# A decoder layer with attention and experts: shared expert and padding rows inside the second stage's last steps, and routing of two batches per operation

## The chip, the cores and the metric

The kernel runs on one core of one Trainium2 chip. The metric is the device time of one execution in microseconds, the median over runs. TensorE (PE), VectorE (DVE), ScalarE (ACT), GpSimd (POOL) and the sync engine (SP, which issues transfers) each work through their own list of instructions in order and wait for each other by semaphores.

## The reference

Sixteen batches of 128 tokens with 256 features go through three blocks, each with a residual and a layer norm: self-attention (linear and windowed, gated), cross-attention with 16 heads on a context of 128 tokens, and a mixture of experts. The last one is what the change is about:

```
logits = tokens @ router_weight.T;  scores = sigmoid(logits);  sfc = scores + router_bias
group_scores = top2 sum of sfc in each of 4 groups of 8 experts;  keep the best 2 groups
topk_idx = top 4 of the kept sfc;  topk_w = scores[topk_idx] / sum * 2.5
mixed  = sum over the 4 chosen experts of topk_w * down(silu(gate(token)) * up(token))
shared = (silu(x @ shared_gate.T) * (x @ shared_up.T)) @ shared_down.T
x = layernorm(x + mixed + shared)
```

There are 32 experts with an inner width of 128; the shared expert has an inner width of 256.

## The kernel before, in words

The program has three stages, with a barrier of all engines and a clearing of semaphores between them. Every float32 product is made of three float16 products (high x high, high x low, low x high), so a value is split into a `_hi` part (a copy by ACT) and a `_lo` part (a subtraction by DVE or POOL).

**Stage 1** (self-attention) is not touched.

**Stage 2** (`cross_attention`) is a software pipeline over the 16 batches (`NB`). Each engine has a loop over steps `i`, and in each step it calls a fixed list of functions, each for the batch `i` minus a lag of its own: the order of this list is the order of the engine's instructions. PE has 23 steps, DVE 21, ACT 23, POOL 25, SP 23; DVE's step i runs together with about PE's step i + 2. A batch's way through the stage: `x1_T`, `q_proj`, `k_proj`, `v_proj`, `scores`, `mins` (a row minimum on DVE, L1333), `exps` (ACT, L1259), `transposed`, `pT_high` and `p_low` (L1339), `weighted`, `out_proj`, `st` (layer norm statistics, DVE, L1379), `pow_` (POOL), `x2` (L1388), then `xhl_high` and `xhl_low`, the transpose `x2_T`, `logits` and `logits_exp` (ACT), and on DVE the routing: `scores_` (L1395 to L1397), `groups` (L1403 to L1407), `picks` (L1414 to L1417), `chosen` (L1425 to L1429, the selection `selc`), `weights` (L1435 to L1439), after PE's `counts` (running numbers within each expert, by a matmul with a triangle of ones) `places` (L1446 to L1448), `slots_` (L1455 to L1458) and `payload` (L1464 to L1467, the last instruction for a batch). POOL then sends the 128 rows of the batch to the memory `x_rows` of the four chosen experts, in four indirect transfers (`scatter`, L1191). Each DVE routing step waits for the one before it through a semaphore (`chain`). ACT uses Exp and Copy here.

PE's products share seven PSUM banks; the table `ORDERS` says who follows whom in each bank, and `Turns.wait` makes PE wait until the previous content of the bank has been read.

**Stage 3** (`expert_layer`). SP first reads the final row of each of the 32 experts from `fill_row` into registers and writes one block of 128 padding rows behind each expert's rows (L1738, 32 transfers from `padrow`). It then waits for the scatters and the pads and gathers blocks of rows `xg` (L1755, 96 tiles, 20 buffers). Meanwhile PE, ACT and DVE compute the shared expert in 8 chunks of two batches (`shared_chunk`): gate and up products over 256 columns (L1934), SiLU on ACT (L1796), the product `shid` (L1867), its halves `sh_hi` (ACT, L1799) and `sh_lo` (DVE, L1871), the down product, and the sum into `xs` (L1876). Between chunk 0 and 1 PE builds with one matmul (L1956) the table which tile belongs to which expert, from a chain of some 19 small DVE instructions (up to L1855). Then come the 96 expert tiles: transposes (L1985), gate and up (L1934 again, 12 matmuls over 128 columns), down (L1995), the weighting on DVE (L1886), an indirect transfer by POOL (L1772), and at the end the final sums and the last layer norm.

## Time and profile before

| | |
|---|---|
| median of 3 runs | 803.7 us (801.82 to 803.7) |
| the profiled execution's own time | 802.68 us |
| its span (first to last instruction) | 800.9 us |
| mean granted TensorE clock | 0.866 of full speed |
| stage 1 | 0 to 270.9 us |
| stage 2 | 270.9 to 557.9 us |
| stage 3: shared expert | 557.9 to 599.2 us |
| stage 3: expert tiles and final sums | 599.2 to 800.9 us |
| PE, DVE, ACT, POOL busy | 78%, 73%, 66%, 67% of the span |

Times in the trace are microseconds from the span's start. An engine's busy time is the union of its instructions' durations; what a row gives in brackets is the idle time of the engine just before it and the instruction that ended it. PEclk is the TensorE clock that was granted, 1.00 for 2.4 GHz and 0.50 for 1.2 GHz, averaged over the stretch.

### The profile page before, as it was taken

How to read it: one execution, taken by the hardware profiler on the slowest of the kernel's cores; microseconds unless marked ns; L12 is line 12 of the kernel's file. 1: busy time of each engine (PE TensorE's matmuls, PEld its weight loads, DVE VectorE, ACT ScalarE, POOL GpSimd, SP SyncE). 2: the span in 40 equal slices, each digit the busy share in tenths (PEclk: the TensorE clock that was granted, in tenths of full speed). 3: DMA queues.
4: the chain of work that ended last, by engine and by line, in shares of the span. 5: the costliest groups of instructions: out<-in, count | busy, mean ns of one | idle time of the engine just before them, and what ended most of it. 6: DMA issues, size and time to landing. Idle time of an engine off the chain costs nothing. (4 is left out here: it accounts for less than half of the span.)

```text
span 800.9 us, 24293 instructions
## 1 busy us (share of the span) xinstructions
PE 624.3 (78%) x7778; PEld 518.9 (65%) x7778; DVE 586.5 (73%) x2170; ACT 524.8 (66%) x1542; POOL 533.2 (67%) x689
## 2 busy tenths in 40 slices
PE   3899999999998488878777888631889999999100
PEld 2688888888888366756666666421679887777100
DVE  5898888888885367999999999882546655555495
ACT  5699999898887299878787787520228765555000
POOL 5877989999898535477767766663004765556684
PEclk9899999999999789787978787655899999999655
DMA  9200000000000122333543354241942555452383
GB/s 323 64 19 2 2 3 14 21 3 3 2 2 4 46 73 68 100 114 115 147 125 119 116 155 129 93 151 55 211 135 79 148 161 154 142 170 85 139 271 117
DMA packets 57131, 77.68 MB, mean 97 GB/s; under 512 B 8488, under 2 KB 46512, under 8 KB 56880
## 3 DMA queue, kind: packets, MB, share of 16 engines
q1 hardware_dynamic: 46208, 56.37, 24.7%
q0 software_dynamic: 7680, 16.87, 5.8%
q10 hardware_dynamic: 3120, 2.88, 1.1%
q8 instruction: 67, 1.10, 0.6%
q14 instruction: 56, 0.46, 0.2%
HBM read 44.39 MB, written 27.49 MB: 90 GB/s over the span
## 5 line engine op out<-in xcount | busy, mean ns | idle before, releaser
L1772 POOL DMA_INDIRECT y_rows<-yo,xg x96 | 94.7, 986 | 98.2 <-DVE yo L1886 60.0
L1886 DVE TENSOR_SCALAR yo<-bank,xg 128x256 f32<-128x256 f32 x96 | 46.4, 484 | 57.2 <-PE bank L1995 56.7
L1259 ACT ACTIVATE scx<-bank,mnx 128x128 f32<-128x128 f32 x256 | 73.9, 408 | 18.9 <-DVE mnx L1333 18.7
L1934 PE MATMUL bank<-gT,we_hi 128*128 128x128 f16 x768 | 79.1, 219 | 4.5 <-DVE eh L1896 3.6
L500 ACT ACTIVATE sc<-sc,mn 128x128 f32<-128x128 f32 x256 | 79.6, 396 | 0.0
L1191 POOL DMA_INDIRECT x_rows<-rows,slot_ix x64 | 63.5, 992 | 21.6 <-issue 18.3
L1162 POOL TENSOR_TENSOR we_lo<-east,we_hi 128x256 f16<-128x256 f32 (+1 forms) x80 | 59.3, 768 | 11.4 <-ACT we_hi L1233 11.1
L1934 PEld LDWEIGHTS bank<-gT,we_hi 128*128 (+1 forms) x768 | 51.8, 96 | 19.9 <-issue 9.9
L674 DVE CUSTOM_DVE_ANT_0 sc<-bank,rel 128x128 f32<-128x128 f32 x256 | 57.8, 286 | 8.7 <-PE bank L783 8.6
L1808 ACT ACTIVATE gT<-bank 128x512 f16<-128x512 f16 x96 | 56.4, 591 | 7.9 <-PE bank L1985 7.7
L1813 ACT ACTIVATE eh_hi<-eh 128x128 f16<-128x128 f32 x96 | 29.7, 309 | 46.8 <-DVE eh L1896 46.2
L1564 PE MATMUL bank<-ident,scx 128*128 128x128 f32 x256 | 51.5, 340 | 2.9 <-ACT scx L1259 2.8
L1934 PE MATMUL bank<-gT,we_lo 128*128 128x128 f16 x384 | 53.1, 218 | 0.0
L1339 DVE TENSOR_TENSOR pTx_lo<-bank,pTx_hi 128x512 f16<-128x512 f32 x64 | 43.6, 681 | 5.2 <-ACT pTx_hi L1267 4.8
L683 DVE TENSOR_TENSOR pT_lo<-bank,pT_hi 128x512 f16<-128x512 f32 x64 | 43.1, 681 | 5.0 <-ACT pT_hi L507 4.9
L830 PE MATMUL bank<-hT,w_hi 128*128 128x128 f16 x384 | 42.6, 227 | 3.3 <-DVE q_lo L655 2.3
L1333 DVE TENSOR_REDUCE mnx<-bank 128x4 f32<-128x512 f32 x64 | 42.5, 673 | 1.1 <-DVE rows L1458 0.3
L507 ACT ACTIVATE pT_hi<-bank 128x512 f16<-128x512 f32 x64 | 37.9, 592 | 6.8 <-PE bank L805 5.0
L1267 ACT ACTIVATE pTx_hi<-bank 128x512 f16<-128x512 f32 x64 | 40.0, 632 | 1.9 <-PE bank L1564 1.8
L793 PE MATMUL bank<-ident,sc 128*128 128x128 f32 x256 | 40.0, 279 | 0.4 <-ACT sc L500 0.4
L1564 PEld LDWEIGHTS bank<-ident,scx 128*128 128x128 f32 x256 | 35.4, 174 | 4.6 <-ACT scx L1259 4.6
L1985 PE MATMUL bank<-ident,xg 128*128 128x128 f16 x384 | 36.6, 218 | 1.6 <-DVE xs L1876 0.8
(291 smaller groups left out, 2441.6 us busy)
## 6 DMA issues: line engine op xcount, KB each, us to landing
xg<-x_rows SPq DMA_DIRECT2D x96, 129.0 KB, 2.6
east<-in_experts SPq DMA_DIRECT2D x32, 384.0 KB, 3.5
rows<-xhl SPq DMA_DIRECT2D x16, 512.0 KB, 4.5
yg<-y_rows SPq DMA_DIRECT2D x16, 512.0 KB, 4.5
x_rows<-padrow SPq DMA_DIRECT2D x33, 129.0 KB, 4.1
wst<-in_wcat SPq DMA_DIRECT2D x8, 256.0 KB, 5.6
cst<-in_ctx_t SPq DMA_DIRECT2D x16, 128.0 KB, 3.3
out<-fin ACTq DMA_DIRECT2D x16, 128.0 KB, 3.1
```

The lines of the kernel that those rows point to most:

```text
L500: done = act.activation(sc[:, g, j], sc[:, g, j], ACT.Exp, bias=mn[:, n % 2, g, j:j + 1], scale=-1.0)
L674: dve.tensor_tensor_reduce(out=sc[:, g, j], in0=sc_bank[g][:, j * P:(j + 1) * P], in1=rel[:, g, j], scale=-1.0, scalar=-NEG, op0=ALU.add, ...
L683: dve.tensor_tensor(pT_lo[:, g % 2], pT_bank[g][:].rearrange("p (h k) -> p h k", h=GH), pT_hi[:, g % 2], ALU.subtract).then_inc(pT_rd[g], 1)
L1162: pool.tensor_tensor(pair(shared.we_lo, piece, n), arrived(piece), pair(shared.we_hi, piece, n), ALU.subtract).then_inc(we_lo_done[k], 1)
L1191: pool.indirect_dma_start(shared.x_rows, bass.IndirectOffsetOnAxis(ap=slot_ix[:, n, k:k + 1], axis=0), rows4[:, q, k], None).then_inc(shar ...
L1259: done = act.activation(scx[:, g, j], sc_bank[g][:, j * P:(j + 1) * P], ACT.Exp, bias=mnx[:, n % 2, g, j:j + 1], scale=-1.0)
L1339: dve.tensor_tensor(pTx_lo[:, g % 2], pT_bank[g][:].rearrange("p (h k) -> p h k", h=GH), pTx_hi[:, g % 2], ALU.subtract).then_inc(xpT_rd[g ...
L1564: last = pe.transpose(pT_bank[g][:, j * P:(j + 1) * P], scx[:, g, j], ident[:])
L1772: pool.indirect_dma_start(c.y_rows, bass.IndirectOffsetOnAxis(ap=xg_word(U32, n % G, 0), axis=0), yo[:, n % YO], None, bounds_check=NDEST ...
L1808: act.activation(gT[:, n % U], GT_BANK[n % len(GT_BANK)], ACT.Copy).then_inc(gt_r, 1)
L1886: dve.tensor_scalar(yo[:, n % YO], DN_BANK[n % 2][:, 0:D], xg_word(F32, n % G, 1), None, ALU.mult).then_inc(yo_r, 1)
L1934: done = pe.matmul(o[:, m * width:(m + 1) * width], lhs(x_, k, m), rhs(y_, k, m), start=t == 0, stop=t == 5)
```

## The change

**Shared expert.** The 8 chunks move from the start of stage 3 into the last steps of stage 2, as functions in the lists of the engines: on PE `sh_in` (gate and up, one batch at a time, so over 128 columns) in steps 17 to 24 and `sh_out` (down) in steps 18 to 25; on ACT `sh_gate` and `sh_high`, on DVE `sh_mult`, `sh_low` and `sh_add`. They use three PSUM banks that other uses leave free by then. `shid`, `sh_hi` and `sh_lo` have one buffer each instead of two. PE's loop now has 26 steps, ACT's 27, DVE's 25, POOL's 26.

**Padding.** `fill_row` is computed on DVE in its step 20, after the last `places`; SP issues 16 of the 32 padding transfers after its loop in stage 2, and ACT the other 16 after its own. SP in stage 3 waits for them before the first gather, as before.

**Routing.** The DVE functions from `scores_` to `payload` run once for two batches, in every second step, with both batches in one instruction where the instruction allows it. MAX8 and MATCH_REPLACE stay one per batch. `counts` on PE does five matmuls per pair instead of four per two batches. `scatter` on POOL runs one step later. The group mask is no longer an operation of its own, and the sum of the weights is.

**Table.** In stage 3, PE's matmul for the tile table now stands in the tile loop, in step 5, ahead of the gate and up product of tile 1 and behind the transposes of tile 4.

Cut to its core:

```diff
-                for i in range(NB + 7):
+                def sh_in(n, b):
+                    if live(n, NCH):
+                        wait_turn(pe, f"GU{b}", n)
+                        for j, col in enumerate((C_SG, C_SU)):
+                            for m in range(KT):
+                                t = 0
+                                for x_, y_ in ((0, 0), (1, 0), (0, 1)):
+                                    for k in range(KT):
+                                        done = pe.matmul(gate_up(b, j)[:, m], W[x_][:, k, col + m * P:col + (m + 1) * P], shared.xT[:, 2 * n + b, y_, k],
+                                                         start=t == 0, stop=t == 5)
+                                        t += 1
+                        done.then_inc(filled[f"GU{b}"], 1)
+                def sh_out(n):
+                    if live(n, NCH):
+                        H = (sh_hi, sh_lo)
+                        wait_turn(pe, "SD", n)
+                        pe.wait_ge(shlo_r, n + 1)
+                        products("SD", lambda s, k, m: H[s][:, m, k], lambda s, k, m: W[s][:, k, C_SD:C_SD + D], 2, D)
+                for i in range(NB + 10):
...
                     x1_T(i)
+                    sh_in(i - FIRST_SH, 0)
                     transposed(i - 3, 0)
                     k_proj(i - 2)
+                    sh_out(i - FIRST_SH - 1)
                     transposed(i - 3, 2)
                     q_proj(i - 1)
+                    sh_in(i - FIRST_SH, 1)
...
+                for i in range(NB + 11):
                     ao_high(i - 6)
                     pT_high(i - 5, 2)
+                    sh_high(i - FIRST_SH - 2)
...
                     x1T_(i - 1)
+                    sh_gate(i - FIRST_SH - 1, 0)
                     xq_high(i - 2)
+                    sh_gate(i - FIRST_SH - 1, 1)
+                pad_rows(act, mybir.EngineType.Activation, 1)
...
-                for i in range(NB + 5):
-                    chosen(i - 5)
+                for i in range(NB + 9):
+                    sh_mult(i - FIRST_SH + 1, 0)
                     xq_low(i)
                     p_low(i - 2, 2)
+                    sh_mult(i - FIRST_SH + 1, 1)
                     xv_low(i - 1)
+                    sh_add(i - FIRST_SH)
                     mins(i - 1, 1)
                     weights(i - 5)
                     places(i - 5)
+                    if i == NB + 4:
+                        dve.tensor_scalar(shared.fill_row[:], shared.count[:], -1.0, None, ALU.add).then_inc(shared.fill_r, 1)
                     mins(i - 1, 0)
+                    sh_low(i - FIRST_SH + 1)
                     scores_(i - 4)
...
+                    chosen(i - 4)
...
+        def pad_rows(eng, kind, part):
+            eng.wait_ge(shared.fill_r, 1)
...
+            for v in rows:
+                eng.dma_start(shared.x_rows[bass.ds(v, P), :], shared.padrow[:]).then_inc(shared.filled, 16)
...
                 def tile(i, s, h):
+                    if i == L_GU + 1:
                         pe.wait_ge(tab_step, TAB_STEPS)
                         pe.matmul(TAB_BANK[:, 0:2 * P], c.ones[:], diag[:].rearrange("p s t -> p (s t)"), start=True, stop=True).then_inc(tab_ps, 1)
```

DVE's list in the steady part of stage 2, where a batch gets its weights (`wraw` to `wt`) and its places (`slots`, `ykey`), before:

```order
L1435 SCALAR_TENSOR_TENSOR wraw,wsum<-cout,score 128x32
L1437 TENSOR_SCALAR wsum<-wsum 128x1
L1438 RECIPROCAL winv<-wsum 128x1
L1439 TENSOR_SCALAR wt<-wraw,winv 128x32
L1446 TENSOR_TENSOR slots<-bank,count 128x32
L1447 TENSOR_TENSOR count<-bank,count 128x32
L1448 TENSOR_TENSOR ykey<-slots,selc 128x32
```

and the same place now, in every second step:

```order
L1485 SCALAR_TENSOR_TENSOR wraw<-cout,score 128x64
L1486 TENSOR_REDUCE wsum<-wraw 128x2
L1487 TENSOR_SCALAR wsum<-wsum 128x2
L1488 RECIPROCAL winv<-wsum 128x2
L1489 SCALAR_TENSOR_TENSOR wt<-wraw,winv 128x64
L1495 TENSOR_TENSOR slots<-bank,count 128x64
L1497 TENSOR_TENSOR count<-bank,count 128x32
L1498 TENSOR_TENSOR ykey<-slots,selc 128x64
```

Seven instructions for each batch have become eight for two, over 64 columns where it was 32.

ACT's list in one of the last steps of stage 2, now (L1328 is the SiLU of the shared expert, L1335 its high half, L1322 the exponential of the logits); before, the stage had no table load:

```order
L1311 ACTIVATE xhl<-xs 128x256
L1328 ACT_TABLE_LOAD
L1328 ACTIVATE shid<-bank 128x256
L1328 ACTIVATE shid<-bank 128x256
L1335 ACTIVATE sh_hi<-shid 128x512
L1316 ACTIVATE hT<-bank 128x512
L1322 ACT_TABLE_LOAD
L1322 ACTIVATE rt_e<-bank 128x32
```

Exp and Silu take turns here. There are nine such loads in the stage's last steps.

PE's list at the start of stage 3, now:

```order
L2016 MATMUL bank<-ident,xg 128x128
L2016 MATMUL bank<-ident,xg 128x128 x3
L1994 MATMUL bank<-diag,ones 128x256
L1984 MATMUL bank<-gT,we_hi 128x128
```

These are the transposes of tile 4, the table's matmul and the first gate product of tile 1; before, the table's matmul stood ahead of the second chunk of the shared expert, and 8 chunks ahead of the first tile.

## Rows read from the trace of the kernel before

**Rows 1.** The page: span

```profile
span 800.9 us, 24293 instructions
```

**Rows 2.** Busy time by stretch (us; engine busy, instructions; PEclk; DMA share; GB/s)

```profile
core 0: us, PE busy (x) PEld busy (x) DVE busy (x) ACT busy (x) POOL busy (x), PEclk, DMA share, GB/s
303.06:315.05 11.99, 10.62 (x144) 8.24 (x141) 8.10 (x19) 11.45 (x36) 7.04 (x12) 0.86 0.30 79
341.44:498.21 156.77, 124.71 (x1466) 99.49 (x1462) 144.42 (x502) 120.16 (x364) 109.28 (x148) 0.79 0.43 129
...
518.00:529.00 11.00, 5.35 (x46) 3.61 (x42) 8.61 (x40) 3.05 (x7) 8.03 (x10) 0.66 0.52 167
529.00:551.00 22.00, 2.82 (x18) 2.39 (x18) 13.94 (x72) 1.21 (x3) 14.86 (x17) 0.50 0.27 96
...
558.00:570.00 12.00, 8.51 (x42) 5.95 (x43) 6.24 (x25) 2.58 (x4) 0.07 (x1) 0.67 0.74 177
570.00:599.00 29.00, 27.52 (x251) 24.14 (x248) 14.66 (x23) 8.45 (x14) 0.00 (x0) 1.00 0.71 167
```

**Rows 3.** DVE in order of time, 487 to 546 (start us, us)

```profile
489.66 0.43 DVE L1379 BATCH_NORM_STATS2 xstats<-bank 128x6 f32<-128x256 f32 x1
...
517.99 0.43 DVE L1379 BATCH_NORM_STATS2 xstats<-bank 128x6 f32<-128x256 f32 x1 [0.77 <-PE bank L1508]
...
528.60 0.43 DVE L1379 BATCH_NORM_STATS2 xstats<-bank 128x6 f32<-128x256 f32 x1 [1.11 <-PE bank L1508]
...
545.26 0.29 DVE L1467 TENSOR_REDUCE rows<-wpick 128x4 f32<-128x128 f32 x1
```

**Rows 4.** In order of time: the ends of stage 2 and of stage 1

```profile
550.15 0.96 POOL L1191 DMA_INDIRECT x_rows<-rows,slot_ix  x1 [0.30 <-issue]
557.94 0.12 POOL L1768 MEMSET cums<- 128x32 f32 x1 [6.83 <-POOLq L963]
...
268.80 0.41 DVE L734 TENSOR_SCALAR xs<-yt,mv,rstd 128x256 f32<-128x256 f32 x1 [0.75 <-POOL rstd L326]
270.94 0.23 POOL L1144 MEMSET xv_hi<- 128x32 f16 x1 [2.18 <-POOLq L946]
```

**Rows 5.** PE in order of time, 566 to 603

```profile
566.43 1.22 PE L1956 MATMUL bank<-diag,ones 128*128 128x256 f32 x2 [3.49 <-DVE diag L1855]
...
572.29 0.60 PE L1934 MATMUL bank<-hT,w_hi 128*128 128x256 f16 x4
...
576.22 0.60 PE L1934 MATMUL bank<-hT,w_hi 128*128 128x256 f16 x4
...
600.62 0.39 PE L1934 MATMUL bank<-gT,we_hi 128*128 128x128 f16 x4
...
601.29 0.39 PE L1985 MATMUL bank<-ident,xg 128*128 128x128 f16 x4
...
602.18 0.39 PE L1985 MATMUL bank<-ident,xg 128*128 128x128 f16 x4
```

**Rows 6.** SP's queue in order of time

```profile
559.71 17.96 SPq L1738 DMA_DIRECT2D x_rows<-padrow  x32
582.55 9.37 SPq L1755 DMA_DIRECT2D xg<-x_rows  x20
```

**Rows 7.** Groups of DVE instructions, 341.44 to 498.21 (busy us, mean ns, idle before)

```profile
L1395 DVE TENSOR_SCALAR rt_e<-rt_e 128x32 f32<-128x32 f32 x10 | 5.6, 560 | 0.0
L1464 DVE TENSOR_TENSOR wpick<-ykey,y 128x128 f32<-128x128 f32 x10 | 5.5, 547 | 0.0
...
L1396 DVE RECIPROCAL score<-rt_e 128x32 f32<-128x32 f32 x10 | 3.5, 353 | 0.3
```

**Rows 8.** In order of time: table load, and the last chunk's low half

```profile
557.94 1.28 ACT L1796 ACT_TABLE_LOAD   x1 [21.33 <-PEq L963]
...
596.20 0.69 DVE L1871 TENSOR_TENSOR sh_lo<-shid,sh_hi 128x512 f16<-128x512 f32 x1 [0.69 <-ACT sh_hi L1799]
```

**Rows 9.** The page: DMA issues (KB each, us to landing)

```profile
xg<-x_rows SPq DMA_DIRECT2D x96, 129.0 KB, 2.6
```

More of the change, by code:

```diff
@@ L31 @@
 PIECES = ((0, 1, 2), (3, 4))
+NCH = NB // 2
+FIRST_SH = 17
 ROUTE_SCALE = 2.5
@@ L81, in live, with pair_done @@
     return 0 <= n < count
+def pair_done(n):
+    return live(n) and n % 2 == 1
 def unrolled(lag, step, count=NB):
@@ L100, in wait @@
                 tile = i + k // len(order) - self.lags[prev]
-                if 0 <= tile < NB:
-                    pe.wait_ge(self.emptied[prev], self.reads.get(prev, 1) * (tile + 1))
+                each = self.every.get(prev, 1)
+                if 0 <= tile < self.counts.get(prev, NB) and (tile + 1) % each == 0:
+                    pe.wait_ge(self.emptied[prev], self.reads.get(prev, 1) * (tile + 1) // each)
                     break
@@ L1106, in arrived @@
             return east[:, k, at:at + 2 * EI * (1 + piece // 4)].rearrange("p (h w) -> p h w", w=2 * EI)
+        def pad_rows(eng, kind, part):
+            eng.wait_ge(shared.fill_r, 1)
+            _, rows = nc.values_load_multi_w_load_instructions(
+                shared.fill_row[0:1, part * NE // 2:(part + 1) * NE // 2], engines=[kind], min_val=0, max_val=NE * CAP - P,
+                skip_runtime_bounds_check_because="an expert's rows start at a multiple of CAP and are at most CAP - P")
+            for v in rows:
+                eng.dma_start(shared.x_rows[bass.ds(v, P), :], shared.padrow[:]).then_inc(shared.filled, 16)
         with nc.Block() as block:
@@ L1138, in _ @@
                     context(i)
+                pad_rows(sp, mybir.EngineType.SP, 0)
             @block.gpsimd
@@ L1204, in _ @@
                     ao_low(i - 5)
-                    scatter(i - 8, 0)
+                    scatter(i - 9, 0)
             @block.scalar
@@ new lines, in places @@
+                def places(n):
+                    if pair_done(n):
+                        link = chain(dve, place_step, PLACE_STEPS, n // 2)
+                        dve.wait_ge(filled["CN"], n // 2 + 1)
+                        link(dve.tensor_tensor(slots[:], room["CN"][:, 0:2 * NE].rearrange("p (s e) -> p s e", s=2),
+                                               shared.count[:].unsqueeze(1).to_broadcast([P, 2, NE]), ALU.add))
+                        dve.tensor_tensor(shared.count[:], room["CN"][:, 2 * NE:3 * NE], shared.count[:], ALU.add).then_inc(emptied["CN"], 1)
+                        link(dve.tensor_tensor(ykey[:], slots[:], selc[:], ALU.mult))
+                        dve.wait_ge(emptied["CN"], n // 2 + 1)
@@ new lines, in slots_ @@
+                def slots_(n):
+                    if pair_done(n):
+                        start = SLOT_STEPS * (n // 2)
+                        for s in range(2):
+                            dve.max(y8[:, s], ykey[:, s]).then_inc(slot_step, 1)
+                        dve.wait_ge(slot_step, start + 2)
+                        dve.tensor_scalar(slot_ix[:, n - 1:n + 1], y8[:, :, 0:TOPK], -1.0, None, ALU.add).then_inc(slot_step, 1)
+                        for b in (n - 1, n):
+                            wait(dve, shared.scattered[b % RR], 16 * TOPK * (b // RR))
+                            dve.tensor_copy(rows4[:, b % RR, :, D:D + 1], dest_f[:, b].unsqueeze(2)).then_inc(slot_step, 1)
@@ new lines, in sh_mult, with sh_low @@
+                def sh_mult(n, b):
+                    if live(n, NCH):
+                        dve.wait_ge(emptied[f"GU{b}"], 2 * n + 1)
+                        dve.tensor_tensor(shid[:, b], gate_up(b, 1), shid[:, b], ALU.mult).then_inc(emptied[f"GU{b}"], 1)
+                def sh_low(n):
+                    if live(n, NCH):
+                        dve.wait_ge(shhi_r, n + 1)
+                        wait(dve, filled["SD"], n)
+                        dve.tensor_tensor(sh_lo[:], shid[:], sh_hi[:], ALU.subtract).then_inc(shlo_r, 1)
@@ L1730, in _ @@
                 sp.dma_start(known[:], consts[:, 2 * P + NE:2 * P + 2 * NE + 1]).then_inc(k_in, 16)
-                sp.wait_ge(fill_r, 1)
-                for half_ in range(2):
-                    _, rows = nc.values_load_multi_w_load_instructions(
-                        fill_row[0:1, half_ * NE // 2:(half_ + 1) * NE // 2], engines=[mybir.EngineType.SP], min_val=0, max_val=NE * CAP - P,
-                        skip_runtime_bounds_check_because="an expert's rows start at a multiple of CAP and are at most CAP - P")
-                    for v in rows:
-                        sp.dma_start(c.x_rows[bass.ds(v, P), :], c.padrow[:]).then_inc(filled, 16)
                 for q in range(RR):
@@ L1827, in _ @@
             def _(dve):
-                dve.tensor_scalar(fill_row[:], c.count[:], -1.0, None, ALU.add).then_inc(fill_r, 1)
                 link = chain(dve, tab_step, TAB_STEPS, 0)
```

264 lines of the change are left out of this document (115 added, 149 removed).

## The prediction

> **What bounds the kernel now.** I read the page first, then the stretches by stage, then in each stage the engine that never waits. The profiled execution took 802.7 us around a span of 800.9 us [rows 1]; the median of the three runs is 803.7 us, so 1 us above what the sums below start from. An effect of 0.3%, 2.4 us, is about what a measurement of this kernel can tell from none.
>
> In the steady part of the second stage DVE is busy 144.4 of 156.8 us, ACT 120.2, PE 124.7, POOL 109.3, and the TensorE clock is granted at 0.79 on average, so PE spends part of it at 1.2 GHz [rows 2]. Ten batches pass there, one per 15.7 us. In the one batch period before any routing (303.06 to 315.05) the time is 12.0 us, DVE busy 8.1 and ACT 11.45 [rows 2]. So two limits are seen: with routing DVE sets 15.7 us, without it ACT sets 12.0 us. DVE's attention work is those 8.1 us, some 7.8 where it runs without a pause and neighbours overlap; the rest of the 15.7 us, 7.9, is routing: 30 small instructions, 0.26 us apiece with the gaps.
>
> The end of that stage is a chain of latencies: PE is busy 5.4 of 11 us, then 2.8 of 22 us, at a clock of 0.66 and 0.50 (1.2 GHz) [rows 2]. Batch 12's statistics start at 489.66, batch 15's at 528.60, the last payload instruction ends at 545.55 [rows 3], POOL's last scatter issues at 550.15, and the third stage starts at 557.94, after 6.83 us of POOL idle [rows 4]. In contrast the first stage ended 269.21 (DVE) and the second began at 270.94, only 1.7 us later [rows 4]; so some 5 of the 6.8 us belong to POOL's indirect transfers being the last thing, not to the barrier.
>
> The third stage begins with the shared expert, which is PE's: 27.5 of 29 us busy at full clock [rows 2], one chunk per 3.93 us (572.29 to 576.22), and the experts' sixth tile (number 5) begins at 602.18, 44.2 us into the stage [rows 5]. The pads (18 us of issue from 559.71) and the first gathers (from 582.55) lie under it [rows 6]. The stage's rest is not touched.
>
> **1. Routing of two batches per operation.** Per pair 60 DVE instructions become 42, since everything except MAX8, MATCH_REPLACE and a few writes is issued once over 64 columns. What goes once instead of twice, by the mean durations [rows 7]: the add after the exponential (0.56 us), the comparison for the payload (0.55), and their like. What gets wider costs by columns: the reciprocal over 64 instead of 32 columns, if proportional, 0.70 for 0.35; the other instructions gain about 0.03 us for 32 columns more. MAX8 stays. Written out for the eight groups (scores 1.6, groups 1.4, picks 1.1, chosen 1.4, weights 1.4, places 0.8, slots 0.9, payload 1.8) a pair costs 10.4 us instead of 15.8; by mere count, 42 at 0.26, it is 11.1. I take 10.8, a saving of 2.5 us per batch, bounds 2.3 and 2.7. The scores to chosen groups fall on one iteration and weights to payload on the next, about 5.4 us each, so there is no heavy and light iteration. DVE's floor becomes 13.2 us per batch, ACT's is 12.0. Two engines that close will wait for each other: I take 13.6 us, a gain of 2.1 us over 11 periods (from batch 4 to the first shared work): **-23 us**. Bounds: nothing below 12.9 us (gain 30), and if coupling eats most, 15 us (gain 8).
>
> **2. The tail.** PE's loop goes from 23 to 26 iterations, with a chunk's gate and up products in iterations 17 to 24 and its down product one later. PE's work per chunk is still 3.9 us at full clock. The gate and up products are now 48 matmuls over 128 columns instead of 24 over 256; the experts do 12 of those in 0.67 us (600.62 to 601.29) [rows 5], thus 2.7 us for 48; a chunk's 36 matmuls over 256 columns took 3.93 us, 0.109 each, thus 2.6 us for the 24. The Trainium skill (TensorE: Matmul & The Clock Gate, Back-to-back issue gap) gives about 81 ns per matmul at 128 columns because each needs its weight load, and by that a chunk would be 1.2 us longer and the tail up to 10 us; the trace has 56 ns here, so the sum goes without it.
>
> The iterations, counted from the statistics of batch 12 (iteration 17): 17 and 18 still carry full attention, plus 4 us of PE work, minus the cheaper routing: 15.5 and 15 us (28.3 for both before, from 489.66 to 517.99 [rows 3]). 19 to 22 carry the last routing chain and a chunk side by side: 13, 10, 9 and 8 (before 10.6, and 17 us for the rest up to 545.55). 23 and 24, and the start of 25, are a chunk's chain alone: sh_low 0.69, out 1.3, gate and up half 1.35, SiLU 0.4, product 0.4, sh_hi about the same as sh_low, and about 1 us of hops: near 6 each (SiLU and product are estimates, half of an operation of sh_low's width and a bit) [rows 5, 8]. Up to the last sh_high that is about 82 us.
>
> ACT must switch between Exp and Silu: nine table loads in the tail where the stage had none, 1.28 us each [rows 8], 11.5 us on an engine that is busy only 3.1 of 11 and 1.2 of 22 us there [rows 2]; about half fall on the chain and are in the iteration times. The Trainium skill (ScalarE: Activation LUTs, What ACT_TABLE_LOAD costs) counts 2.66 us for a switch with its drain, and advises to group work by set, against this change; by it the tail would be another 6 us longer. The trace's own load stands alone at the stage's start, 1.28 us and then a wait for PE, so it shows no drain; 6 us more stay inside the forecast's own range.
>
> The padding rows: their numbers exist after the last count (DVE iteration 20). SP has nothing left and issues 16 in 9 us under chunks 5 to 7, at 17.96/32 = 0.56 us apiece with the register loads [rows 6]. ACT's 16 stand behind its last sh_high and nothing covers them: 16 x 0.56 = **9 us**, taking ACT to issue as fast as SP, while sh_low, the down product and the add need 3. So ACT ends the stage, 82 + 0.6 + 9, about 92 us after batch 12's statistics. POOL scatters batches 14 and 15 together, 8 x (0.96 + 0.30) = 10 us [rows 4], plus its 5 us of draining, but starts at about 66 and is done by 82: hidden, so the exit costs 2 us and not 6.8. Tail: 94 us against 68.3 now: **+26 us**. Bounds +16 (iterations near 6 us from 20 on) and +42.
>
> **3. The third stage's head.** No shared expert, and no wait for the pads. SP gathers at once; landing takes 2.6 us [rows 9]. But PE now waits before tile 5 for the table that DVE builds: its matmul started 8.5 us into the stage, and takes 1.2 us [rows 5]. So tile 5 begins at 9.7 us instead of 44.2: -34.5. PE comes out of a pause and has the 1.2 GHz clock for the first 8 us or more, as it had from 558 to 569 (mean 0.67 up to 570, then 1.00 [rows 2]); tiles of 1.2 us then take 2.4: +4. **-30.6 us**, bounds -27 and -34. Gathers go out every 0.47 us (9.37/20) [rows 6] and stay ahead.
>
> Sum: 802.7 - 23 + 26 - 30.6 = **775 us**.
>
> **Rivals.**
> *Coupling keeps the period near 15.* For it: ACT is at 12.0 us per batch, PE at 12.5 with half its time at the low clock, POOL at 11 with in-order scatters; against it: the 12.0 us period with ACT at 95%. Gain 8 instead of 23: 790 us. Chance 0.17.
> *Clock in the tail stays at 1.2 GHz.* For it: 0.66 and 0.50 there [rows 2]. Each chunk's 2.7 us in the chain double; over the last iterations +10: 785 us. Against: added matmuls make PE denser. Chance 0.15.
> *Both cheap.* Period 13.0 (-30) and a tail of +20: 762 us. Chance 0.10.
> *Slower: the tail runs serially.* ACT and DVE are in-order queues, and one waiting SiLU holds the routing behind it. If a chunk's chain (5.8, with slow clock 8.5) and two table loads (2.6) add fully to iterations 17 to 22, 67 us, and three bare chunks follow at 8.5, then the tail is 55.9 + 67 + 25.5 + 11.5 = 159 us for 68.3, and the kernel 840 us. It decides from 54 us of growth instead of 26, or 3.1 us more in each of nine iterations. Against it: ACT and PE are nearly idle there, and chunks are put one iteration apart. Chance 0.06, and 0.02 for just balancing.
> *Forecast, 766 to 784*: 0.50.
>
> **How the numbers follow.** Time 775 us, the likeliest case. Range 760 to 793: it takes in the first three rivals and leaves out the serial one and the extreme of the cheap one. Faster 0.92, same 0.02, slower 0.06, since only the serial case brings back the 54 us of steps 1 and 3.
>
> **What would show it.** Right: statistics of neighbouring batches 13 to 14 us apart between 340 and 480; DVE waiting at times, for ACT or PE; the third stage starting at about 557.9 - 23 + 26 = 561; ACT's pad issues last before it, with POOL idle; the experts' sixth tile under 15 us after the stage's start. Wrong: a period over 15, table-load pairs with ACT full in the tail, stage start after 575, or a first gather that waits for the pads.

## The result and the profile after

The changed kernel takes 769.79 us (768.49 to 772.76, 4 runs) against 802.88 us (801.82 to 803.7, 4 runs) for the kernel before: a ratio of 0.9594, 95% interval 0.9561 to 0.9626. The forecast was 775 us, the range 760 to 793. All ratios leave out two runs far from the others, one of the kernel before (1775.5 us) and one of the routing alone (909.07 us, clock 0.70). The profiled execution took 770.42 us around a span of 768.6 us:

```profile
span 768.6 us, 24515 instructions
```

Busy time by stretch of the changed kernel: the steady part, four stretches of the tail up to the last payload, the chunks alone, the wait for the pads, and the third stage's head. They answer to [rows 2].

```profile
core 0: us, PE busy (x) PEld busy (x) DVE busy (x) ACT busy (x) POOL busy (x), PEclk, DMA share, GB/s
343.50:469.80 126.30, 102.11 (x1356) 82.63 (x1358) 112.71 (x353) 109.32 (x335) 96.09 (x129) 0.92 0.46 139
469.80:488.80 19.00, 15.25 (x188) 12.54 (x186) 13.96 (x53) 15.49 (x41) 13.58 (x19) 0.80 0.45 140
488.80:505.60 16.80, 14.08 (x170) 12.33 (x170) 10.86 (x27) 11.73 (x29) 7.86 (x10) 0.72 0.25 79
505.60:517.00 11.40, 8.60 (x109) 7.41 (x108) 8.95 (x44) 6.97 (x13) 6.98 (x10) 0.92 0.37 118
517.00:535.80 18.80, 15.46 (x184) 13.89 (x183) 15.24 (x68) 8.12 (x13) 12.46 (x14) 0.87 0.37 131
535.80:549.00 13.20, 9.36 (x140) 8.62 (x136) 5.58 (x11) 3.81 (x8) 7.85 (x8) 1.00 1.01 228
549.00:559.70 10.70, 1.47 (x12) 1.10 (x12) 1.38 (x2) 0.00 (x0) 0.00 (x0) 0.83 0.87 193
559.70:570.20 10.50, 5.38 (x46) 4.59 (x47) 5.17 (x23) 2.85 (x6) 0.12 (x1) 0.52 0.69 172
```

In the steady part DVE is busy 89% (before 92%) and ACT 87% (before 77%): no engine is full any more. The tail, where PE was busy 2.8 of 22 us, now has PE at four fifths, and the 1.2 GHz clock (0.50) is gone from it. At the very end nearly nothing computes for 10.7 us while the transfer engines stay at 0.87.

The same by instructions in order of time, as [rows 3]: DVE's statistics of batches 13, 14 and 15, the last payload instruction, and the last addition of the shared expert.

```profile
488.83 0.43 DVE L1421 BATCH_NORM_STATS2 xstats<-bank 128x6 f32<-128x256 f32 x1 [0.28 <-PE bank L1585]
505.62 0.43 DVE L1421 BATCH_NORM_STATS2 xstats<-bank 128x6 f32<-128x256 f32 x1
517.01 0.43 DVE L1421 BATCH_NORM_STATS2 xstats<-bank 128x6 f32<-128x256 f32 x1 [0.60 <-PE bank L1585]
535.27 0.48 DVE L1521 TENSOR_REDUCE rows<-wpick 128x4 f32<-128x128 f32 x2
551.37 0.69 DVE L1537 TENSOR_TENSOR xs<-bank,xs 128x512 f32<-128x512 f32 x1 [1.65 <-PE bank L1585]
```

POOL's, ACT's and SP's queues around the border of the stages, as [rows 4, 6]:

```profile
545.59 0.96 POOL L1216 DMA_INDIRECT x_rows<-rows,slot_ix  x1 [0.31 <-issue]
559.70 0.12 POOL L1851 MEMSET cums<- 128x32 f32 x1 [13.16 <-POOLq L971]
...
549.77 8.16 ACTq L1130 DMA_DIRECT2D x_rows<-padrow  x16
...
534.71 9.05 SPq L1130 DMA_DIRECT2D x_rows<-padrow  x16
562.65 10.08 SPq L1838 DMA_DIRECT2D xg<-x_rows  x20
```

And PE at the start of stage 3, as [rows 5]: the transposes of tiles 0 to 3, the table's matmul, and tile 5.

```profile
564.82 2.07 PE L2016 MATMUL bank<-ident,xg 128*128 128x128 f16 x16 [13.49 <-DMA xg<-x_rows]
...
568.39 1.17 PE L1994 MATMUL bank<-diag,ones 128*128 128x256 f32 x2
...
570.22 0.39 PE L2016 MATMUL bank<-ident,xg 128*128 128x128 f16 x4
```

With the statistics of batch 12 at 469.80 (before 489.66), the span divides as follows (us). The first two result columns are the profiled executions of the kernel before and of the changed one; the two after them are the parts alone, of the experiments below.

| stretch | before | changed | routing alone | shared expert alone |
|---|---|---|---|---|
| up to the statistics of batch 12 | 489.7 | 469.8 | 468.9 | 488.1 |
| from there to batch 15's | 38.9 | 47.2 | 41.2 | 49.9 |
| from there to stage 3 | 29.3 | 42.7 | 33.4 | 44.8 |
| stage 3 up to tile 5 | 44.2 | 10.5 | 43.0 | 10.0 |
| the rest | 198.7 | 198.4 | 199.1 | 198.5 |

So -19.9, then +21.7 in the tail (from batch 12's statistics to stage 3), then -33.7 in the head (stage 3 up to tile 5): 32 us.

### The profile page after: what moved, and what is told of

Its sections match the earlier page's. It is cut to its first block and busy times, and to the rows that moved or that the text cites. A ratio compares the mean times of both kernels' runs of the same rounds, so it can differ in the third digit from the quotient of the medians.

```text
span 768.6 us, 24515 instructions
## 1 busy us (share of the span) xinstructions
PE 610.7 (79%) x7986; PEld 513.5 (67%) x7986; DVE 552.5 (72%) x2018; ACT 534.4 (70%) x1558; POOL 534.5 (70%) x689
## 5 line engine op out<-in xcount | busy, mean ns | idle before, releaser
L1936 DVE TENSOR_SCALAR yo<-bank,xg 128x256 f32<-128x256 f32 x96 | 46.4, 484 | 57.1 <-PE bank L2028 57.0
L1187 POOL TENSOR_TENSOR we_lo<-east,we_hi 128x256 f16<-128x256 f32 (+1 forms) x80 | 59.5, 769 | 11.7 <-ACT we_hi L1258 11.5
L1381 DVE TENSOR_TENSOR pTx_lo<-bank,pTx_hi 128x512 f16<-128x512 f32 x64 | 43.7, 682 | 10.5 <-ACT pTx_hi L1292 10.4
L1641 PE MATMUL bank<-ident,scx 128*128 128x128 f32 x256 | 46.4, 311 | 2.9 <-ACT scx L1284 2.3
L2016 PEld LDWEIGHTS bank<-ident,xg 128*128 128x128 f16 x384 | 24.4, 98 | 18.2 <-DMA xg<-x_rows 14.1
```

Of the source, the lines that this page charges most:

```text
L1187: pool.tensor_tensor(pair(shared.we_lo, piece, n), arrived(piece), pair(shared.we_hi, piece, n), ALU.subtract).then_inc(we_lo_done[k], 1)
L1381: dve.tensor_tensor(pTx_lo[:, g % 2], pT_bank[g][:].rearrange("p (h k) -> p h k", h=GH), pTx_hi[:, g % 2], ALU.subtract).then_inc(xpT_rd[g ...
L1641: last = pe.transpose(pT_bank[g][:, j * P:(j + 1) * P], scx[:, g, j], ident[:])
L1936: dve.tensor_scalar(yo[:, n % YO], DN_BANK[n % 2][:, 0:D], xg_word(F32, n % G, 1), None, ALU.mult).then_inc(yo_r, 1)
L2016: done = pe.transpose(GT_BANK[n % len(GT_BANK)][:, part, k], xg[:].bitcast(F16)[:, n % G, (part * KT + k) * P:(part * KT + k + 1) * P], c. ...
```

## The experiments

Twelve kernels ran, in three groups. The first four ran on a chip where the kernel before takes 801.03 us; the next four and the last four on two other chips, where it takes 865.93 and 865.83 us. The record does not name the chip of the result above; the kernel before takes 802.88 us there, and "the first chip" below means both. Between those chips and the first only ratios, or differences within a group, are compared. Each diff is against the changed kernel unless it says otherwise.

### Each part alone

The first kernel has the paired routing alone (no `sh_` functions, pads and shared expert in stage 3 as before), the second the move of the shared expert, pads and table alone (routing per batch).

```diff
-                    sh_in(i - FIRST_SH, 0)
-                    sh_out(i - FIRST_SH - 1)
-                    sh_in(i - FIRST_SH, 1)
...
-                pad_rows(sp, mybir.EngineType.SP, 0)
...
-                pad_rows(act, mybir.EngineType.Activation, 1)
```

and the second:

```diff
-                    if pair_done(n):
-                        link = chain(dve, score_step, SCORE_STEPS, n // 2)
+                    if live(n):
+                        s = n % 2
+                        link = chain(dve, score_step, SCORE_STEPS, n)
```

> Only the routing of two batches per operation, shared expert and pads where they were. My theory (DVE sets the steady period, so its saving is time): the period falls from 15.7 to about 13.8 us as in the changed kernel, batch 12's statistics come some 20 us earlier; at the end POOL has eight scatters behind the last payload instead of four (8 x 1.26 instead of 4 x 1.26 us), which gives back about 4.5 us of it: 803 - 20 + 4.5 = 787 us. Rival A (the gain of the steady part needs the rest of the change, or is lost again in the stage's end): 797 us or more. Rival B (no loss at the end): 783.

> Only the move of the shared expert, the pads and the tile table; routing one batch at a time. My theory (the two parts add): stage 3's head gains 33.7 us as in the changed kernel, the stage's end grows by about 24 us (21.6 measured with pairs, and some 2.5 us more of DVE work in each of a few iterations, less the four scatters that POOL has less): 803 - 33.7 + 24 = 793 us, with batch 12's statistics still at about 489.7. Rival (the chunks only fit because paired routing made room on DVE): the end grows by 34 us or more, 803 us or slower.

Measured: routing alone 788.38 us, ratio 0.9851 (0.9824 to 0.9877); shared expert alone 795.04 us, ratio 0.9924 (0.9895 to 0.9953). Both are near what was expected, and they save 12.6 and 6.0 us, 19 together, where the whole change saves 33. The table above shows where the parts don't add. Routing alone makes the tail 6.4 us longer than before, shared expert alone makes it 26.5 longer: 33 together, but the whole change pays only 22. The end of the routing alone, by stretch:

```profile
468.90:486.70 17.80, 14.74 (x140) 11.43 (x138) 12.66 (x51) 11.87 (x36) 13.58 (x19) 0.62 0.47 150
486.70:498.60 11.90, 10.32 (x107) 7.88 (x104) 8.62 (x23) 8.03 (x24) 7.25 (x10) 0.50 0.33 104
498.60:510.10 11.50, 6.69 (x53) 4.96 (x50) 7.50 (x41) 3.05 (x7) 8.46 (x11) 0.50 0.44 145
510.10:526.00 15.90, 3.22 (x20) 2.80 (x20) 11.03 (x58) 1.21 (x3) 11.35 (x13) 0.50 0.39 132
```

PE runs at or near 1.2 GHz (0.50) throughout; the kernel before had 0.84, 0.50, 0.66 and 0.50 in its four stretches between the same instructions. Also its last eight scatters, of two batches, come after the last payload (526.03 to 536.64, stage 3 at 543.48) and hold the exit; before, they ended 5.6 us after it. In the whole change they lie under the chunks. From this I took the slow clock to be the cause of the longer end, and tested it (below).

### The table loads

```diff
-                        act.activation(shid[:, b], gate_up(b, 0), ACT.Silu).then_inc(emptied[f"GU{b}"], 1)
+                        act.activation(shid[:, b], gate_up(b, 0), ACT.Copy).then_inc(emptied[f"GU{b}"], 1)
```

The shared expert's SiLU is left out, so ACT needs no table but that of Exp, and the nine loads are gone.

> The changed kernel with a plain copy for the SiLU of the shared expert, in the same places and widths (this leaves out the shared expert's SiLU): no change of tables in the second stage, one load at the start of the third. My theory (nine loads of 1.28 us, about half of them on the chain): 770 - 5.5 = 764 us. Rival A, by the Trainium skill (ScalarE: Activation LUTs, What ACT_TABLE_LOAD costs: 2.66 us per switch with its drain): 11 us or more less, 759. Rival B (ACT waits there anyway, loads are hidden): 770.

Measured: 769.49 us, ratio 0.9615 (0.9579 to 0.9651), for 0.9594 (0.9561 to 0.9626) with the loads. The nine loads together cost nothing that can be measured; by the two intervals the cost is at most some 2 us, so the 5.5 us of the theory are excluded, a load or two on the chain is not. One of the loads in the changed kernel, on ACT:

```profile
502.42 0.59 ACT L1304 ACTIVATE aT<-bank 128x512 f16<-128x512 f16 x1
503.02 1.28 ACT L1322 ACT_TABLE_LOAD   x1
504.32 0.20 ACT L1322 ACTIVATE rt_e<-bank 128x32 f32<-128x32 f32 x1
```

The load starts at the end of the instruction before it, takes 1.28 us, and the next one follows at once; no drain beside it is seen, so the 2.66 us of the Trainium skill (ScalarE: Activation LUTs, What ACT_TABLE_LOAD costs) are not what this trace shows. This load is on the chain that ended last, which the profile follows back to 499.48 and which goes from ACT's `aT` through the load to the exponential and DVE's routing:

```profile
503.02 0.36 ACT L1322
```

It is the only one of the six loads after 499.48 that the chain touches. The others fall where something else was later; ACT is busy 42.3 of the 66.0 us from batch 12's statistics to the last payload, with the loads. The traces agree on the size: from batch 12's statistics to the end of the last `sh_high` it is 79.2 us with the loads and 78.0 without.

### Who issues the padding

```diff
+                pad_rows(sp, mybir.EngineType.SP, 1)
-                pad_rows(act, mybir.EngineType.Activation, 1)
```

> The changed kernel with all 32 padding transfers on SP (16 more behind its own 16) and none on ACT. My theory (ACT's issue behind its last work ends the stage): ACT's 16 issues end at 557.93, DVE's last add at 552.06; SP's issues would run from 534.7 to about 552.7, so the third stage starts at about 554.5 instead of 559.7, and the table chain, not the gathers, sets its start: 770 - 5 = 765 us. Rival (the DMA engines, fully busy from 536 to 549, land the pads no earlier, and the first gather still waits for them until about 562): 769 to 770 us, stage 3 starting earlier but its first tile not.

Measured: 767.49 us, ratio 0.9582 (0.9536 to 0.9628), between the two expectations and indistinguishable from the changed kernel. SP issued all 32 from 535.35 to 555.36 (0.62 us each instead of 0.57), stage 3 began 2.2 us earlier, but SP still waited until 560.95 for the landing, so the first gather left only 1.7 us earlier. The chain that ended last in the changed kernel says the same from its side: PE's last chunk, then ACT's pad issues (left out here), then the landing of pads, then the first gather.

```profile
544.59 1.47 PE bank L1585 x12
546.07 1.35 PE bank L1705 x24
...
557.59 4.98 DMA x_rows<-padrow
562.65 2.13 DMA xg<-x_rows
```

The pads back in stage 3, all on SP after the barrier:

```diff
-                pad_rows(sp, mybir.EngineType.SP, 0)
...
-                pad_rows(act, mybir.EngineType.Activation, 1)
...
+                sp.wait_ge(c.fill_r, 1)
+                for half_ in range(2):
...
+                    for v in rows:
+                        sp.dma_start(c.x_rows[bass.ds(v, P), :], c.padrow[:]).then_inc(c.filled, 16)
```

> The changed kernel with all 32 padding transfers back at the start of stage 3, on SP; the shared expert stays in stage 2. Theory (the pads must leave stage 3 with the shared expert that hid them): stage 3 starts about 5 us earlier, at 554, since ACT issues nothing after its last work; then 18 us of issue and 5 us of landing stand alone before the first gather, at about 578; tile 5 begins near 585 instead of 570: 769 + 14 = 783 us. Rival (gathers overlap the pads enough, or the table chain hides most): under 776.

Measured on the second chip: 862.46 us, ratio 0.9962 (0.9946 to 0.9979): almost the whole gain is gone, somewhat more than expected. Stage 3 begins at 583.69, the pads take SP from 585.47 to 603.46, the first gather leaves at 609.80 and tile 5 begins at 617.23, 33.5 us into the stage. Without the shared expert over them, pads in stage 3 stand bare; the move of the pads is what makes the move of the shared expert pay.

Pads split 26 to 6, with two semaphores (the first 16 gathers wait for the first 16 pads), and `known` loaded in stage 2:

```diff
-                pad_rows(sp, mybir.EngineType.SP, 0)
+                pad_rows(sp, mybir.EngineType.SP, 0, 16)
+                pad_rows(sp, mybir.EngineType.SP, 16, 26)
...
-                pad_rows(act, mybir.EngineType.Activation, 1)
+                pad_rows(act, mybir.EngineType.Activation, 26, 32)
...
-                sp.wait_ge(c.filled, 16 * NE)
+                sp.wait_ge(c.filled[0], 16 * 16)
...
+                    if n == 16:
+                        sp.wait_ge(c.filled[1], 16 * 16)
```

> A version meant to beat the change: SP issues 26 of the pads and ACT 6; two semaphores, so that the first 16 gathers (first blocks of experts 0 to 15) wait for the pads of these 16 experts alone; and the constants of the table are loaded in stage 2. Theory (ACT's issue and the wait for landed pads are on the path): stage 3 starts at about 555 instead of 559.7, gathers go out at once, the table is ready 5.5 us into the stage instead of 8.5, and tile 5 begins at about 563 instead of 570.2: 769 - 7 = 762 us. Rival, after e4 (the DMA engines' rate is the limit, gathers queue behind the pads): first tiles land near 562 as before, 767 us.

Measured on the second chip: 836.25 us, ratio 0.9685 (0.9653 to 0.9718). There was no run of the changed kernel beside it, so it was run again in the last group.

### Does DVE still set the period?

```diff
-                        dve.tensor_tensor(wpick[:], ykey[:].unsqueeze(2).to_broadcast([P, 2, TOPK, NE]),
-                                          y8[:, :, 0:TOPK].unsqueeze(3).to_broadcast([P, 2, TOPK, NE]), ALU.is_equal).then_inc(pay_step, 1)
...
-                        dve.tensor_tensor(wpick[:], wpick[:], wt[:].unsqueeze(2).to_broadcast([P, 2, TOPK, NE]), ALU.mult).then_inc(pay_step, 1)
```

> The changed kernel without the two products of the payload step (comparison and weighting, 0.50 + 0.81 us per pair); the tokens' weights in the rows are then something else. It asks what sets the steady period now. Theory 1 (DVE still does): the period falls by 0.65 us from 13.8 to 13.1, batch 12's statistics come 7 us earlier: 762 us. Theory 2 (ACT, with 12.5 of 13.8 us busy, and the waits between ACT, DVE and POOL do): 2 us or less, 767 or more.

This kernel leaves out the comparison and the weighting, so the weights that go with the tokens are wrong. Measured on the second chip: 846.02 us, ratio 0.9786 (0.9759 to 0.9812), the statistics of batch 12 at 484.2, as in the two kernels before it (485.9 and 483.7). Removing 1.3 us of DVE work per pair gives nothing there: the statistics stand 15.1 and 16.0 us apart in turn with it and without. The same steady stretch, of this kernel:

```profile
359.00:470.40 111.40, 87.93 (x1057) 73.10 (x1058) 86.34 (x289) 84.08 (x257) 79.62 (x110) 0.79 0.42 127
```

DVE is busy 78% there, ACT 75%, PE 79% at a granted clock of 0.79. On the first chip the changed kernel has a period of 13.75 us and a clock of 0.92. So on the second chip DVE does not bound this part; that PE does so through its clock fits, but wasn't tested, and on the first chip this kernel did not run. What sets the period of 13.75 us there was not tested either.

### Is it the clock that makes the end slow?

The paired routing alone, with idle products of the shared expert's shape in PE's steps from 17 on (their results are read by nobody). Against the routing alone:

```diff
+                def filler(i):
+                    if i >= 17:
+                        for j, col in enumerate((C_SG, C_SU)):
...
+                                        pe.matmul(room["XT"][:, j * D:j * D + P], W[x_][:, k, col + m * P:col + (m + 1) * P], shared.xT[:, i - 17, y_, k],
+                                                   start=t == 0, stop=t == 11)
...
+                    filler(i)
```

> Paired routing alone (e1) with idle matmuls: in PE's steps 17 to 22 twice 24 matmuls over 128 columns whose result nobody reads, as much work as the gate and up products of a chunk. My theory, new: in e1 the clock falls to 1.2 GHz from 469 us on (0.62, then 0.50) and what DVE waits for there is PE; the shared expert's work in the changed kernel holds the clock at 0.72 to 0.92. Then the filler's own 2.7 us per step are paid back by the clock: granted clock over 0.75 in the stage's end, time from batch 12's to batch 15's statistics 38 us or less instead of 41.2, whole kernel 3 us or more faster than e1 (788), at 785 or less. Rival (latencies between engines make the end, the clock does not matter): the added work comes on top, 790 us or more.

Measured on the second chip: 854.99 us, ratio 0.9873 (0.9825 to 0.992), with no run of the routing alone beside it. It too was run again.

### The last group: four kernels side by side, on a third chip

The changed kernel, the routing alone, the routing alone with idle products, and the split pads, all unaltered.

> The changed kernel once more, unaltered, beside the three kernels that follow, so that all stand on one chip. Theory (the gain has three terms: batch period -1.9 us in twelve batches, tail +22, head of stage 3 -34): a ratio to the kernel before of 0.955 to 0.965 on a chip like the first. Rival, should this be a chip on which the tensor engine rather than the vector engine sets the batch period (as in the group before this one, where the period was 15.5 us with the paired routing): the period term is then half as large and the ratio 0.97 to 0.98.

> The paired routing alone, once more. Theory (what the paired routing gains in the steady part, 20.8 us, it gives back in part at the end of stage 2, where with little work for the tensor engine its granted clock falls to 0.50): batches 12 to 15 again 41 us apart and the way from batch 15's statistics to stage 3 again 33 us, with a granted clock under 0.6 there, ratio near 0.985. Rival (those 6.4 us were an accident of the one profile): 39 and 29 us, ratio 0.975 or less.

> The paired routing alone with idle products of the shared expert's shape in the tensor engine's last six steps (results are thrown away). Theory (the clock is what makes the end of the paired routing slow, and the shared expert's products cure it by keeping the engine busy): granted clock above 0.75 in the end, the stretch from batch 12 to stage 3 is at least 3 us shorter than in the paired routing alone, and the ratio at least 0.004 below its ratio. Rival (the end is a chain of vector-engine, transfer and gather steps in which the clock hardly counts, and the idle products only stand in the way): clock up, stretch equal or longer, ratio equal or higher.

> The changed kernel with 26 padding transfers on the sync engine and 6 on the scalar engine, two semaphores for them (the first gathers wait for half of them) and the table of stage 3's first step loaded in stage 2. Theory (after the last addition the changed kernel waits only for the padding and then for its landing, some 7.6 us to the end of the stage and 3 us in stage 3, of which the split takes most of the first): 4 to 7 us shorter than the changed kernel on the same chip, ratio between the two 0.991 to 0.995. Rival (the transfers' rate decides, 1.0 of the engines' time is taken while they run, so whoever issues them the first gather starts no earlier): within 2 us of the changed kernel.

| kernel | median us | ratio (95%) |
|---|---|---|
| changed kernel | 844.21 | 0.9737 (0.9709 to 0.9766) |
| routing alone | 844.8 | 0.9769 (0.9742 to 0.9795) |
| routing alone, idle products | 853.21 | 0.9855 (0.983 to 0.9881) |
| changed kernel, split pads | 838.53 | 0.9695 (0.9672 to 0.9718) |

The changed kernel came out as its rival had it (0.97 to 0.98), not the theory. The routing alone lies between its two expectations: 39.0 us from batch 12 to batch 15, as the rival had it, and 33.4 from there to stage 3, as the theory had it.

**The clock** is not the cure: the idle products raise it, and the kernel gets 8 us slower. The last four stretches (from batch 12's statistics to the last payload), first without and then with them:

```profile
483.30:498.80 15.50, 11.17 (x135) 9.09 (x136) 12.44 (x50) 10.49 (x34) 10.85 (x15) 0.87 0.49 154
498.80:510.90 12.10, 9.15 (x95) 7.24 (x92) 8.71 (x25) 8.83 (x26) 7.41 (x10) 0.50 0.34 107
510.90:522.30 11.40, 6.54 (x48) 4.82 (x44) 7.43 (x40) 3.05 (x7) 8.33 (x11) 0.50 0.43 142
522.30:538.30 16.00, 3.22 (x20) 2.80 (x20) 11.08 (x58) 1.21 (x3) 11.35 (x13) 0.50 0.39 132
```

```profile
486.00:503.30 17.30, 13.53 (x186) 11.77 (x186) 12.89 (x51) 10.57 (x34) 10.89 (x15) 0.90 0.44 139
503.30:517.30 14.00, 10.64 (x134) 10.05 (x134) 8.71 (x25) 8.80 (x26) 7.12 (x10) 0.76 0.27 86
517.30:529.60 12.30, 9.78 (x96) 9.05 (x97) 7.55 (x41) 3.21 (x8) 8.63 (x11) 0.65 0.44 140
529.60:548.90 19.30, 13.53 (x159) 12.02 (x158) 11.19 (x58) 1.21 (x3) 11.35 (x13) 0.77 0.32 111
```

The clock goes from 0.50 to between 0.65 and 0.77 in the last three, and each of the four is 0.9 to 3.3 us longer. The likely reason is that the products stand in PE's queue in front of what the chain needs, and cost more than the clock gives back; PE is busy 47.5 us there instead of 30.1. My theory that the shared expert helps the routing's end by keeping the clock up is not borne out by this. What is shown is that in the whole change the tail is 11 us shorter than the two parts' tails together, and the traces of the first chip place all of it. The scatters at the end, hidden under the chunks, are 5 us (5.6 us from last payload to last scatter before, 10.6 with the routing alone). The other 6 us lie between batch 12's statistics and the last payload: pairing the routing makes this stretch 1.2 us longer without the chunks (55.9 to 57.1) and 4.6 us shorter with them (70.6 to 66.0). It takes 8.3 us of DVE's work out in both cases; without the chunks DVE waits longer instead (3.3 us before, 14.9 with the routing alone). That the chunks turn the saved work into time because DVE has their work to do fits this, and was not tested by a run.

**The change is worth less on this chip**, and the routing has nearly all of it (844.8 against 844.2, ratios with intervals that overlap). By stretches, from routing alone to the changed kernel: up to batch 12 +3.4 us, to stage 3 +32.5 (72.4 to 104.9), to tile 5 -35.4 (45.4 to 10.0), rest +0.7. On the first chip the same two kernels give +0.9, +15.3 (74.6 to 89.9), -32.5 and -0.7. So the head pays the same everywhere, and what varies is what the shared expert adds to the tail. What slows these chips wasn't found: in the expert tiles the same instructions take the same time, but the rest from tile 5 takes 242 us for 198. The trace places a part of it on PE: in 100 us of those tiles its weight loads stand 31.9 us without anything in the profile that they wait for, 8.7 us on the first chip. No trace of the kernel before was taken on these chips, so where the routing alone gains its 21 us there (12.6 on the first) can't be said.

**The split pads win**: the mean of the five runs is 4.9 us below the changed kernel's, with 2.9 us of uncertainty (95%) by their scatter; the ratio between the two is 0.994, as expected. The queues around the border, first of the changed kernel on this chip and then with the split:

```profile
559.38 9.46 SPq L1130 DMA_DIRECT2D x_rows<-padrow  x16
581.83 7.97 ACTq L1130 DMA_DIRECT2D x_rows<-padrow  x16
591.61 0.12 POOL L1851 MEMSET cums<- 128x32 f32 x1 [20.12 <-POOLq L971]
```

```profile
556.36 17.49 SPq L1131 DMA_DIRECT2D x_rows<-padrow  x26
579.09 2.93 ACTq L1131 DMA_DIRECT2D x_rows<-padrow  x6
583.79 0.12 POOL L1854 MEMSET cums<- 128x32 f32 x1 [15.29 <-POOLq L972]
```

The SP queue is idle for 13 us in the first, between its 16 pads and ACT's; in the second it carries ten of them there. From the last payload to stage 3 it is 31.2 us and 26.4, and the first gather leaves 2.5 and 0.5 us into the stage: 6.8 us in the traces. This version beats both kernels on this chip. On the first it wasn't run; there the transfers were at 1.01 of the engines' time in the chunks, and all pads on SP gave no more than 2 us. What the split, the two semaphores and the early load of `known` give each was not separated by runs; 4.8 of the 6.8 us lie before stage 3, where only the split acts.

## Why the prediction was right

**1. The routing.** Forecast -23 us up to batch 12, measured -19.9. The period was right: 13.6 us forecast, 13.75 measured from batch 4 to batch 12. What failed is the count: "11 periods (from batch 4 to the first shared work)"; only eight lie between 359.8 and 469.8. They gained 2.05 us each, 16.4 together, batch 3 to 4 gained 3.1 (15.6 us before, 12.5 now), and 0.4 came earlier. The period itself is right in part by luck, since two errors cancel in it. DVE's floor was forecast at 13.2 us and the rest for waiting at 0.4; over the eight periods DVE is busy 99.59 us, 12.45 for each, and the period lies 1.3 above that:

```profile
359.79:469.80 110.01, 88.14 (x1190) 71.71 (x1187) 99.59 (x320) 95.83 (x293) 87.99 (x119) 0.92 0.48 144
```

DVE's routing takes about 10 us per pair, 10.8 forecast. The groups that answer to [rows 7], now over 64 or 256 columns and once per pair:

```profile
L1437 DVE RECIPROCAL score<-rt_e 128x64 f32<-128x64 f32 x5 | 2.8, 553 | 0.2
L1515 DVE TENSOR_TENSOR wpick<-ykey,y 128x256 f32<-128x256 f32 x5 | 2.6, 512 | 0.0
...
L1436 DVE TENSOR_SCALAR rt_e<-rt_e 128x64 f32<-128x64 f32 x5 | 1.4, 284 | 1.0 <-ACT rt_e L1322 0.9
```

The reciprocal took 0.55 us for 64 columns where proportion said 0.70. The comparison over 256 columns took 0.51 us where one over 128 had taken 0.55, and the addition over 64 took 0.28 for 0.56 over 32. Those means were no measure of the instructions, since POOL's work beside them stretches them. Two additions of the kernel before, one beside POOL and one not:

```profile
425.00 1.92 POOL L1162 TENSOR_TENSOR we_lo<-east,we_hi 128x256 f16<-128x256 f32 x3
425.11 0.62 DVE L1395 TENSOR_SCALAR rt_e<-rt_e 128x32 f32<-128x32 f32 x1
...
488.84 0.17 DVE L1395 TENSOR_SCALAR rt_e<-rt_e 128x32 f32<-128x32 f32 x1
```

Where POOL does not compute, the addition over 64 columns takes 0.20 us for 0.17 over 32, and the comparison over 256 takes 0.42 for 0.28 over 128. That "there is no heavy and light iteration" was wrong: the statistics stand 12.4 and 15.3 us apart in turn.

**2. The tail.** Forecast +26, measured +21.7 (bounds +16 and +42). Iterations 17 and 18 took 19.0 and 16.8 us, not 15.5 and 15: full attention and a chunk don't fit beside each other that well, with PE busy 15.3 of 19 at a clock of 0.80. From there all was cheaper: iteration 19 took 11.4 for 13. A chunk alone takes 5.27 us, not 6, ACT in order of time:

```profile
539.27 0.38 ACT L1328 ACTIVATE shid<-bank 128x256 f32<-128x256 f32 x1 [0.82 <-DVE sh_lo L1532]
...
544.54 0.38 ACT L1328 ACTIVATE shid<-bank 128x256 f32<-128x256 f32 x1 [0.82 <-DVE sh_lo L1532]
```

The chunk is a closed loop: gate and up of one batch (24 matmuls in 1.35 us, 56 ns each, by the chain above), the down product (1.47), SiLU, product, both halves, and again, since `shid` and its halves have one buffer. The last `sh_high` ends 79.2 us after batch 12's statistics, 82 forecast; ACT's pads take 8.2 us of issue, 9 forecast; the exit 1.8 us from ACT's last issue to stage 3, 2 forecast. The step "about half fall on the chain", of the table loads, is wrong: one does as far as the chain is traced, 1.3 us of 11.5. The 56 ns per matmul of 128 columns, taken from the experts' products, held; the 81 ns of the Trainium skill (TensorE: Matmul & The Clock Gate, Back-to-back issue gap) would have made each 24 take 1.9 us, and in the chunks alone, at a clock of 1.00, no such row stands (24 of them took 2.16 us once, at 516.97, at a clock of 0.64).

**3. The head.** Forecast -30.6, measured -33.7. The table's matmul runs 8.7 us into the stage (8.5 forecast). "A first gather that waits for the pads" was listed as a sign of being wrong, and it does wait: SP stands from 559.70 to 562.65 for pads that ACT had issued last. It costs little, since the table's DVE chain ended at 567.85, half a microsecond before PE was at its matmul. What failed is "+4" for the 1.2 GHz clock after the pause: the clock is 0.52 up to tile 5, but those tiles lie beside the table's chain, and from tile 5 to the end the kernel takes 198.4 us where it took 198.7.

**The rivals.** Coupling keeps no period of 15 on the first chip. On the two others the period is 15.5 to 15.8 us, as that rival had it, but its gain of 8 us is not what they show: the routing alone gains 21 us on the third. The clock in the tail did not stay at 1.2 GHz. The tail was far from serial: 89.9 us, where that rival had 159. The sum came out 4.6 us above the profiled execution: step 1 promised 3 us too much, steps 2 and 3 were 4 and 3 us too cautious. That they cancel in part is luck. The mechanism of steps 2 and 3 held; for step 1 the routing alone shows that pairing shortens the period, and that DVE still sets it on the first chip stays argued.

## What to carry to other kernels

Work that fills waits is cheap as long as it enters a stretch in which its engine idles, and dear in the steps that are still full: place it where the queues are thin, and take along what stood under it, or that stands bare (pads left behind cost 19 us of 23 here by ratios from two chips, and 16 us against the kernel without the payload's products on the same chip). Parts of a change need not add: one part's loss can be another's cover, so test them alone and together. A split of transfers between two queues should follow when each queue is free, not halve the number. And before the mean of a small instruction goes into a sum, look at its single rows: a part of the mean can belong to a neighbour.

## What was not expected of the hardware

- The same kernel differs by 8% between groups of runs: the kernel before takes 803 us on one chip and 866 on two others, with equal durations of single instructions in the expert tiles; the change gives 4.1% on the first and 2.6% (0.9737) on the third. Each chip ran at one time only, so chip and hour can't be told apart.
- POOL's last indirect transfer, 5.6 us after the payload before, held the exit for 6.8 us [rows 4], and with the routing alone it did so again on two chips (6.8 us each); with the chunks behind it the exit took 1.8 us.
- A small DVE instruction takes more than three times as long while POOL computes. Of the 16 additions over 32 columns in the kernel before, nine lie under a TENSOR_TENSOR of POOL and took 0.61 to 0.64 us, six do not and took 0.17 or 0.18, and the one that POOL reached before its end took 0.48. In three of the six POOL was issuing an indirect transfer, which does not stretch them (0.18). Of the 16 comparisons over 128 columns, five without POOL's work took 0.28 or 0.29 us, ten beside it 0.42 to 1.09; the last (at 521.67) took 0.28 and POOL's operation beside it 0.82 instead of 0.67. This is read from the trace; no kernel without POOL's work was run.
